# Layer kernel on one core: side work of the attention steps put in other steps, two more half groups of exponentials on VectorE, last output projection as fp32r parts

## Time and profile before

| | |
|---|---|
| median of 3 runs | 595.82 us (595.65 to 595.88) |
| the profiled execution | 596.11 us |
| its span, first to last instruction | 594.1 us |
| PE (TensorE) busy | 584.3 us, 98% |
| ACT (ScalarE) busy | 505.2 us, 85% |
| DVE (VectorE) busy | 459.2 us, 77% |
| POOL (GpSimd) busy | 47.4 us, 8% |
| granted clock of TensorE | 0.998 |

### The profile page before, as it was taken

How to read it: one execution, slowest core, us unless ns; L and a number is a source line. 1 busy time by engine, 2 the same in 40 slices (tenths; PEclk the granted TensorE clock), 3 DMA queues, 4 the chain that set the end, 5 groups by cost and what they waited for, 6 DMA issues and landing times.

```text
span 594.1 us, 10873 instructions
## 1 busy us (share of the span) xinstructions
PE 584.3 (98%) x4096; PEld 247.8 (42%) x4096; DVE 459.2 (77%) x836; ACT 505.2 (85%) x614; POOL 47.4 (8%) x47
## 2 busy tenths in 40 slices
PE   8999999999999999999999999999999999999995
PEld 7884222222222223223222322222222227988875
DVE  6678888989888867687686668888868696686875
ACT  4539999999999999999999999999999995163352
POOL 6600000000000000000000000003000001102023
PEclk9999999999999999999999999999999999999999
DMA  9466948212303020111211010111010000101102
GB/s 219 61 107 84 126 63 105 29 26 35 86 11 70 8 34 9 31 15 26 62 16 29 11 30 11 30 46 32 9 32 7 7 5 8 41 1 36 36 1 71
DMA packets 36185, 24.72 MB, mean 42 GB/s; under 512 B 24930, under 2 KB 30946, under 8 KB 35538
## 3 DMA queue, kind: packets, MB, share of 16 engines
q1 hardware_dynamic: 34740, 23.29, 23.0%
q10 hardware_dynamic: 1392, 0.72, 0.5%
HBM read 6.56 MB, written 4.33 MB: 18 GB/s over the span
## 4 chain that ended last, share of the span: by engine, by line
PE 97%; DVE 1%; DMA 0%; issue 0%; ACT 0%; POOL 0%; POOLq 0%
PE ps L1289 42%; PE ps L1261 29%; PE ps L1362 10%; PE ps L1131 6%; PE ps L1394 5%; PE ps L1316 2%; PE ps L1102 1%; DVE attn_q L834 1%; PE ps L1336 1%; PE ps L1117 1%; PE ps L1319 1%; DMA out<-out_tmp 0%; DVE xt_lo L736 0%; PE ps L1163 0%; DVE neg_mean L1076 0%
## 5 line engine op out<-in xcount | busy, mean ns | idle before, releaser
L668 ACT ACTIVATE probs<-ps 128x1024 f32<-128x1024 f32 (+1 forms) x512 | 442.9, 1093 | 12.0 <-PE ps L1261 11.6
L1289 PE MATMUL ps<-probs,v_all 128*17 128x512 f32 x1910 | 268.9, 598 | 0.9
L1261 PE MATMUL ps<-q_slot,k_stack 51*128 51x512 f32 x1024 | 196.4, 456 | 0.0
L1261 PEld LDWEIGHTS ps<-q_slot,k_stack 51*128 51x128 f32 x1024 | 84.4, 184 | 219.2 <-ACT probs L668 204.6
L908 DVE TENSOR_SCALAR bits<-ps 128x512 int32<-128x512 f32 x69 | 47.5, 689 | 32.6 <-PE ps L1261 31.3
L1289 PE MATMUL ps<-poly,v_all 128*17 128x512 f32 x138 | 71.3, 598 | 0.0
L687 ACT ACTIVATE sg<-ps,sgate_c 128x512 f32<-128x512 f32 x32 | 22.0, 688 | 49.3 <-PE ps L1362 49.3
L1289 PEld LDWEIGHTS ps<-probs,v_all 128*17 128x17 f32 x1910 | 33.6, 95 | 59.9 <-issue 45.8
L932 DVE SCALAR_TENSOR_TENSOR poly<-poly,bits 128x512 f32<-128x512 f32 x69 | 49.3, 714 | 7.2
L928 DVE SCALAR_TENSOR_TENSOR poly<-poly,mant 128x512 f32<-128x512 f32 x69 | 47.7, 692 | 2.4
L919 DVE SCALAR_TENSOR_TENSOR poly<-mant 128x512 f32<-128x512 f32 x69 | 47.2, 684 | 0.0
(11 more groups left out here) (101 smaller groups left out, 447.9 us busy)
## 6 DMA issues: line engine op xcount, KB each, us to landing
q_slot<-qy SPq DMA_DIRECT2D x64, 64.0 KB
k_stack<-k_part SPq DMA_DIRECT2D x12, 256.0 KB
at_dram<-attn_q SPq DMA_DIRECT2D x64, 34.0 KB
at<-at_dram SPq DMA_DIRECT2D x8, 272.0 KB, 2.9
q_slot<-qy SPq DMA_DIRECT2D x64, 32.0 KB
x_tok<-in_L_attn_X SPq DMA_DIRECT2D x14, 128.0 KB, 5.6
k_stack<-k_part SPq DMA_DIRECT2D x12, 128.0 KB
out<-out_tmp SPq DMA_DIRECT2D x12, 128.0 KB, 2.2
```

The lines of the kernel that those rows point to most:

```text
L668: nc.scalar.activation(probs[:, slot_of(g), first:2, :].rearrange("p a b -> p (a b)"), ps[:, 2 * ring + first:2 * ring + 2, :].rearrange(" ...
L1261: last = nc.tensor.matmul(ps[:, 2 * ring + half, :], k_stack[s % QUADS][base:base + ROWS, p, kt * P:(kt + 1) * P], q_slot[slot][base:base ...
L1289: last = nc.tensor.matmul(ps[32 * hh:32 * hh + VW, ACC, :], v_all[:, tiles[hh], NQ * (s % QUADS) + hh, :], prob, start=(kt == 0), stop=(kt ...
```

## The change

`poly_tiles` gives five tiles also to steps 7 and 11. `scale_attn(c)` stays in stage 1 for chunk 0; for chunks 1 and 2 it goes to stage 0, behind the fourth polynomial of the step. `ln1_add(c, 0)` goes from stage 2, behind the first polynomial, to stage 1, behind the fourth; `ln1_add(c, 1)` from stage 3 to stage 2, behind the third; `ln1_stats` and `ln1_variance` from stage 3 to stage 2, behind the fourth; `ln1_scale` stays in stage 3, but behind the second polynomial instead of at the end. The output projections move to units 8 and 12 of stage 1 and 1 and 8 of stage 2 (chunk 0), and to 3 and 10 of stage 1 and 1 and 8 of stage 2 (chunks 1 and 2). For the last chunk VectorE makes fp32r high and low parts of Wo and of at32 (`split_out`, four instructions), and TensorE multiplies three combinations of them (`project_last`, 24 matmuls).

```diff
+            return [2, 5, 8, 11, 14] if s <= QUADS or s % QUADS == QUADS - 1 and s < STEPS - 1 else [2, 6, 10, 13]
...
+            def split_out():
+                dve.wait_ge(pv_done, UPS * STEPS)
+                nc.vector.tensor_copy(wo_hi[:], wo[:]).then_inc(out_hi_ready, 1)
+                dve.wait_ge(attn_scaled, CH)
+                nc.vector.tensor_copy(at_hi[:], at32[:, :, 0:HD, :]).then_inc(out_hi_ready, 1)
+                dve.wait_ge(out_hi_ready, 1)
+                nc.vector.tensor_tensor(wo_lo[:], wo[:], wo_hi[:].bitcast(f32), ALU.subtract).then_inc(out_ready, 1)
+                dve.wait_ge(out_hi_ready, 2)
+                nc.vector.tensor_tensor(at_lo[:], at32[:, :, 0:HD, :], at_hi[:].bitcast(f32), ALU.subtract
+                                        ).then_inc(out_ready, 1)
...
                 exponentials(tiles[0])
-                if c >= 0 and stage == 1:
+                if c == 0 and stage == 1:
                     scale_attn(c)
-                if c >= 0 and stage == 2:
-                    ln1_add(c, 0)
-                if c >= 0 and stage == 3:
-                    ln1_add(c, 1)
...
                 if c >= 0 and stage == 3:
-                    ln1_stats(c)
+                    ln1_scale(c)
...
                 exponentials(tiles[2])
-                if c >= 0 and stage == 3:
+                if c >= 0 and stage == 2:
+                    ln1_add(c, 1)
+                exponentials(tiles[3])
+                if c >= 0 and stage == 2:
+                    ln1_stats(c)
                     ln1_variance(c)
-                for n in tiles[3:]:
+                if c >= 1 and stage == 0:
+                    scale_attn(c)
+                if c >= 0 and stage == 1:
+                    ln1_add(c, 0)
+                for n in tiles[4:]:
                     exponentials(n)
-                if c >= 0 and stage == 3:
-                    ln1_scale(c)
...
                     scale_attn(LAST)
+                    split_out()
...
+            def project_last():
+                pe.wait_ge(out_ready, 2)
+                pe.wait_ge(gate_up_free, MT)
+                terms = [(x, w, ko) for x, w in ((at_hi, wo_hi), (at_lo, wo_hi), (at_hi, wo_lo)) for ko in range(KO)]
+                for j in range(TPC):
+                    half = j % 2
+                    for n, (x, w, ko) in enumerate(terms):
+                        last = nc.tensor.matmul(ps[:, out_bank(LAST, j // 2), half * HID:(half + 1) * HID],
+                                                x[:, ko, CH * j:CH * (j + 1), :].rearrange("p d u -> p (d u)"),
+                                                w[:, ko, :], start=(n == 0), stop=(n == len(terms) - 1))
+                    if half:
+                        last.then_inc(wo_psum, 1)
...
+            OUT_AT = [(1, 8), (1, 12), (2, 1), (2, 8)], [(1, 3), (1, 10), (2, 1), (2, 8)]
...
-                if c >= 0 and stage in (1, 2) and kt in (8, 15):
-                    project_out(c, 2 * (stage - 1) + kt // 15)
+                if c >= 0 and (stage, kt) in OUT_AT[c > 0]:
+                    project_out(c, OUT_AT[c > 0].index((stage, kt)))
...
-                    for j in range(TPC):
-                        project_out(LAST, j)
+                    project_last()
```

More of the change, by code:

```diff
@@ L149, in layer_program @@
         probs = place("probs", [P, HALVES + 1, 2, CW], f32, at)
+        at_hi = place("at_hi", [P, KO, HD, UW], f32r, at)
+        at_lo = place("at_lo", [P, KO, HD, UW], f32r, at + 4 * KB)
+        wo_hi = place("wo_hi", [P, KO, HID], f32r, at + 8 * KB)
+        wo_lo = place("wo_lo", [P, KO, HID], f32r, at + 10 * KB)
         at32 = place("at32", [P, KO, VW, UW], f32, at + 24 * KB)
@@ L222, in layer_program @@
         attn_scaled = sem("attn_scaled")
+        out_hi_ready = sem("out_hi_ready")
+        out_ready = sem("out_ready")
         ffn_w_ready = sem("ffn_w_ready")
@@ L316, in poly_tiles @@
         def poly_tiles(s):
-            return [2, 5, 8, 11, 14] if s <= QUADS else [2, 6, 10, 13]
+            return [2, 5, 8, 11, 14] if s <= QUADS or s % QUADS == QUADS - 1 and s < STEPS - 1 else [2, 6, 10, 13]
         def value_order(s):
@@ L1299, in project_out @@
                     pe.wait_ge(w_loaded[3], 16)
-                if j == 0 and c == LAST:
-                    pe.wait_ge(gate_up_free, MT)
-                elif j == 0 and c:
+                elif j == 0:
                     pe.wait_ge(yt_ready, KO * c)
-                if j == 2 and c < LAST:
+                if j == 2:
                     pe.wait_ge(ln1_sum, 2 * c + 1)
@@ L1311, in project_out @@
                 for ko in range(KO):
[L1314 to L1320, removed]
+                    for d in range(CH):
+                        last = nc.tensor.matmul(dst[UW * d:UW * (d + 1), :], at32[:, ko, CH * j + d, :], wo[:, ko, :],
+                                                start=(ko == 0), stop=(ko == KO - 1))
                 if half:
                     last.then_inc(wo_psum, 1)
+            def project_last():
[10 more added lines that the diff above has]
+                        last.then_inc(wo_psum, 1)
             def turn_y(c, ko):
```

## The result

The changed kernel takes 598.91 us (median of 6 runs, 598.50 to 599.24). Of the six runs of the kernel before that were timed beside it one took 634.88 us; the other five took 595.65 to 596.63, median 595.88. The ratio is 1.0049, with a 95% interval of 1.0038 to 1.0059: slower by half a per cent, some 3 us, where I had forecast 1.07 us more and a range that ended at 598.2. The profiled execution took 599.24 us, its span 597.2 instead of 594.1.

The account below looks back on a forecast made before the run. TensorE was taken to pace steps with two projections, ScalarE's exponentials those without. Terms -0.67 + 0 - 0.20 + 0 + 0.75 + 1.19 = +1.07 us on the profiled 596.11, less 0.29 for the median: 596.9, range 595.0 to 598.2.

Parts of the forecast that it names:

- the hidden bubbles: Projection at unit 1 of stage 2: TensorE's 0.225 us wait at the border goes, three times, -0.67; bounds -0.67 and 0.
- the other places of the projections: Projections at the remaining moved units: same count and price, so 0, with 0.5 us to either side.
- The five half groups: Five polynomials in steps 7 and 11: relief of ScalarE, -0.1 us each, -0.2 together; bounds -0.5 and +0.6.
- rival D: Steps 7 and 11: delayed polynomials stop TensorE, not made good, both steps over 27.6; +0.8 us against the sum, 597.7; 9%.
- The late third polynomial: Steps 7 and 11: ln1_scale makes the third polynomial start about 1.0 us late, stopping TensorE for about 0.5.
- Step 12: scale_attn's product waits for GpSimd's second cast, save_attn 1.07 us late; less 0.32 of ScalarE's cost in step 13: +0.75.
- The last projection: After attention: TensorE starts 1.77 us later behind four split instructions, its matmuls take 0.58 less: +1.19.
- rival A: Split before the last projection: VectorE's copies go at one element per cycle, +0.78 us, 597.7; 18%.
- Rival B: Step 12: scale_attn isn't held up by GpSimd's second cast, -0.75 us, 596.1; 14%.
- rival C: Attention steps: relief of ScalarE is worth more, steps give 1.67 us instead of 0.87, 596.1; 14%.

Follow-up runs that it names:

- The lighter exponentials: Kernel before with ScalarE's exponentials for 448 of each 512 columns from step 5 on, projections at old places or moved as in the places alone: 591.77 and 590.91 us.
- the places alone: Kernel before with projections at units 8 and 12 of stage 1, 1 and 8 of stage 2, first addition at stage 1's end: 596.71 us, ratio 1.0017.
- the last experiment: Kernel before with five half groups in steps 7, 11, 15, second addition to variance in stage 2, last projection from parts behind unit 9's gate_up: 594.73 us, ratio 0.9982.

## Why the prediction was wrong

**The step that failed: the places of the projections.** I had -0.67 for the hidden bubbles and 0 for "the other places of the projections", with 0.5 to either side and 0 as the border's upper bound. Together they measure +0.93 when done alone, 1.6 above the sum's terms and outside their bounds; that is most of the 2 us by which the forecast is too low. The mechanism was named ("in which ScalarE paces"), and its size was wrong; the two lines should have been one. I took a projection out of one place and put it in another at the same price, and left the waits of the units behind it as they were.

The traces show what it does. A projection costs TensorE 0.86 wherever it stands, but the units behind it then don't wait for ScalarE, until TensorE has caught up with it again; it can be ahead by no more than the ring of three pairs. In the kernel before, the one at unit 8 of stage 1 already spares units 9 to 14 their waits. Moved from unit 15 to 12, the next one has nothing more to spare there. Taken out of the end of stage 2, a projection gives back only half of its 0.86: units 0, 1, 5 and 6 of stage 3 wait 0.43 again. And at the border 0.1 of the 0.22 is waited for ScalarE after all. The lighter exponentials show the cause: with ScalarE out of the way the sum's -0.67 comes out as -0.68.

**The five half groups** were put at -0.20, and measure -0.18. That is luck, for it is +0.65 and -0.83: the whole gain was 0.42 for each, not 0.25, and the late polynomials of rival D took most of it back, in step 11 0.17 and in step 7, with the pause that stays unexplained, 0.50. Rival D's sign, both steps over 27.6, came in step 7 alone. I had the gain from two steps with different neighbours, 27.20 and 27.45. The late third polynomial is where I had it: it stops TensorE for 0.40, and I had put about 0.5.

**Step 12** was right in its mechanism and in the delay: `save_attn` 1.07 late, 1.05 measured by moving the casts. The 0.32 that I took off again, because ScalarE's share of step 13 would be made good, did not come: with and without the collision step 13 has the same waits besides. The term was +0.75 and is +1.05.

**The last projection** was +1.19 and measures +1.1; rival A, copies at one element per cycle, is refuted by 0.42 and 0.69. (The pace between the rows of 512 and 1024 elements is 1.04 ns an element and not 1.06, which changes nothing.) That rule of the Trainium skill (VectorE: DVE Perf Modes, "The perf-mode tier table") holds for a copy from fp32 to fp32r too: 0.42 and 0.69 beside 0.68 and 1.22 for the differences.

The sum by what was measured: +0.93 - 0.18 + 1.05 + 1.1 = 2.9, against 3.1 in the spans. The 0.2 left lies in steps 9 and 13, with the places 3 and 10 of chunks 1 and 2: with four half groups they last 28.78 and 28.76, and 28.68 with the places 8 and 12. There the projection at unit 10 stands behind a wait of 0.2, and the one at the border loses 0.1 more. Step 8 lasts 27.98 both in the changed kernel and with the places alone, which leave `scale_attn` in stage 1, so moving that costs nothing there. The places 3 and 10 were not tried by themselves. Rival B (no collision) and rival C (more relief) are refuted for the changed kernel; C's relief was there, but D used most of it up and the places brought a loss.

## What to carry to other kernels

Where two engines hand work to each other through a short ring and are nearly balanced, cost filler work by stretches. Filler costs its length where it stands, but where the other engine paces it spares the waits behind it, so taking it out of such a stretch gains only a part (here half), and putting it close behind other filler spares nothing more. Relief of the other engine is worth its full price in a stretch without filler (0.42 here) and nothing in one where filler has already spared the waits, so place it by the stretch and not by the engine's idle time. An instruction sequence that stands between two engines costs most of its length beyond the slack in front of it, however small its share of busy time. So look first for other work of the waiting engine that can stand in front of the wait: in the last experiment that took the wait away, though no shorter time came of it.

## What the runs showed of the hardware

An exponential of 128 x 1024 shows 1.0 to 1.3 us in the trace, but ScalarE starts one every 0.90 us; the records overlap. Behind a half one the next starts after 0.48, and the difference, 0.42, is what a half group gives where ScalarE paces. I had not used this. GpSimd's cast holds a VectorE product with two tensors in SBUF until about its own end: 2.33 instead of 1.23 us. The reciprocals, with one tensor in SBUF, took 0.54 in the same place, as without a cast.
